# Attention's prelude in a transformer block on one core: one value product and early queries in the output product's bank, and the last chunk's row statistics in later slots

## The chip, the cores and the metric

One Trainium2 chip, one of its cores. The metric is the device time of one launch in microseconds (us), the median of several runs.

## The reference

```python
x = x + 0.5 * ffn(layernorm(x))          # x: 8 x 512 rows of 128
x = x + attn(layernorm(x))
x = x + 0.5 * ffn(layernorm(x))

def attn(x):                              # 16 heads of 64, causal; adds its own input
    q, k, v = x @ Wq, x @ Wk, x @ Wv
    s = q @ k^T / 8, masked above the diagonal
    return x + (softmax(s) @ v) @ Wo
```

`ffn` is a mixture of 32 experts (6 chosen for a row) with 16 anchors and one shared expert. The same FFN weights serve both FFN layers.

## The kernel before

The 4096 rows are worked as 8 chunks (`NC`) of 512 rows, and a chunk of 512 is one sequence of the attention. The whole is in float32 accuracy: a product is three matmuls, high part times high part, high times low and low times high (`mm3`, lines 197 to 199). A product's result in PSUM is therefore split: ScalarE writes the high part (`part_hi`, line 781, tiles `q_hi` and `k_hi`), then VectorE the low part (`part_lo`, line 1205 for `k_lo`, line 1201 for `q_lo`). Each engine has its program written out by hand, and semaphores join them.

The program is `ffn(0)`, `attention()`, `ffn(NC)`. Attention is a prelude and then 64 slots, one for each pair of heads (8 pairs in each of 8 chunks). Slot (b, p) works on several pairs at once. TensorE (PE) does, in this order:

- transposes of pair p-1's probabilities, group 1 (`probT`, line 505);
- scores of pair p+1, parts 0 and 1 (`scores`, lines 484 and 494); in their last part, behind `third_ready`, PE waits for copies of group 1;
- transposes of pair p-1, group 2;
- the keys' product of pair p+2 (K, into bank `psA`), the value product p+3 (V, into a bank of `psT`), pair p-2's output product (`project_out`, line 532, into bank `psO`), the queries' product of pair p+2 (Q, into `psA`);
- scores of pair p+1, part 2, and transposes of pair p, group 0;
- `attend` for pair p-1 (line 519, into `psA`).

The order in which the others serve this is fixed too. ScalarE (ACT) copies `psA` and half of the transposes (lines 825 and 814), makes `k_hi`, the exponentials of part 0 (`exp`, line 803), the value copy (`value_copy`, line 789), `q_hi`, and the exponentials of parts 1 and 2. VectorE (DVE) copies transposes (`pT_copy`, line 1227), takes the reciprocal of the row sums (line 1220; GpSimd then normalises, line 1358, and PE transposes), the row maxima of parts 0 and 1 (`row_max`, line 1212), `k_lo`, `q_lo`, the row maximum of part 2, and the copy of group 0.

`scores` of part u can be written when the exponentials of the part that used its banks last are done: parts share two bank pairs, so pair 1's part 1 waits for pair 0's part 2.

The prelude on PE makes the value product 0 (`psA`), K of pair 1 (bank 0 of `psT`), scores part 2 of pair 0, Q of pair 1 (bank 1 of `psT`), and then value products 1 and 2, both into `psA`, each behind the copy of the one before:

```python
                for k in (1, 2):
                    pe.wait_ge(s["v_sb"], k)
                    project_values(0, k, psA)
```

`psO` is the last bank. The FFN's last transposes lie in it until VectorE has added them (`add_y`, line 1111, semaphore `x_added`); then nothing uses it until the first output product in slot 2.

The rows' layernorm needs 1/sqrt(var + eps). In attention, the statistics of the last chunk can only be made after `add_y`: VectorE makes them in slot 0 (lines 946 to 960), ScalarE takes a square root in slot 1 (`row_std(4)`, line 690), and VectorE refines in slot 2 (`finish_std`, lines 905 to 916). A square root and an exponential need different tables on ScalarE, and the program loads a table (ACT_TABLE_LOAD) before each change. Late in attention, in chunk 5, VectorE makes such a root alone for other rows, with a seed and Newton steps (`rsqrt_seed` and `rsqrt_newton`, lines 923 to 937).

Of the kernel before, what the change touches and what calls it, by code (L numbers as in the profile page):

```python
# [32 lines left out]
TB = 4  # L33
# [12 lines left out]
RSQRT_SEED = 0x5f3759df  # L46
HP = H // 2
# [22 lines left out]
def build(nc, x_in, wg_in, wu_in, wd_in, gate_in, bias_in, wq_in, wk_in, wv_in, wo_in,  # L70
# [6 lines left out]
    with ctx:  # L77
# [171 lines left out]

        def ahead(b, p, d):  # L250

            return b + (p + d) // HP, (p + d) % HP

# [4 lines left out]
        def transposed(p, g, h=slice(0, 2)):  # L258
# [6 lines left out]
        STD = [(0, 1, 1), (1, 2, 2), (2, NC, NC), (0, NC - 1, 2 * NC - 1), (NC - 1, NC, 2 * NC),  # L265
               (2, NC, 3 * NC)]
# [82 lines left out]
        def _(pe):  # L349
# [189 lines left out]
            def attn_slot(b, p, parity, first, last):  # L539
# [29 lines left out]

                second_ready()  # L570
                if not (first and p == 0):
                    probT(*ahead(b, p, -1), 1)
                if have_s:
                    scores(*ahead(b, p, 1), 0, False)
                    scores(*ahead(b, p, 1), 1, False, third_ready)
                else:
                    third_ready()
# [66 lines left out]
            def attention():  # L644
# [40 lines left out]
        def _(act):  # L685
# [69 lines left out]
            def ffn(g0):  # L755
                ffn_chunk(g0, True, False, 2 if g0 == 0 else 5)
# [18 lines left out]
            def part_hi(b, p, which, early, special=False):  # L775
# [5 lines left out]
                nc.scalar.activation(qk[which][0][:, p % 2, :], psT[:, 1 - which, :] if early else psT[:, 1, :] if special else psA,  # L781
                                     ACT.Copy, scale=(float(DK) ** -0.5, 1.0)[which]) \
                    .then_inc(s[("q_hi", "k_hi")[which]], 1)
# [43 lines left out]
            def attn_slot(b, p, first, last):  # L827
# [22 lines left out]
                if have_q and special:  # L850
                    part_hi(*ahead(b, p, 2), 1, False, True)
# [7 lines left out]
                if p == 1 and first:  # L859
                    row_std(4)  # L860

            def attention():
# [36 lines left out]
        def _(dve):  # L899
# [20 lines left out]
            def rsqrt_seed(c):  # L920
# [3 lines left out]
                dve.wait_ge(s["rsqrt"], 1)  # L924
# [3 lines left out]
            def rsqrt_newton(c, i, last):  # L928
# [3 lines left out]
                dve.wait_ge(s["rsqrt"], 2 + 3 * i)  # L932
                tt(t, y, y, ALU.mult).then_inc(s["rsqrt"], 1)
                dve.wait_ge(s["rsqrt"], 3 + 3 * i)
                stt(out=t, in0=t, scalar=-0.5, in1=v, op0=ALU.mult, op1=ALU.mult).then_inc(s["rsqrt"], 1)
                dve.wait_ge(s["rsqrt"], 4 + 3 * i)
# [177 lines left out]
            def ffn_chunk(g, g0, first, last):  # L1114
# [50 lines left out]
                if first:  # L1165
                    finish_std(2 if g0 == 0 else 5)
# [10 lines left out]
            def a_rows(b, first, ts):  # L1177

                if not first and ts[0] == 0:
                    dve.wait_ge(s["a_xT_ps"], b)  # L1180
                normalise(b, "a_xn", ts)
# [12 lines left out]
            def part_lo(b, p, which, early, special=False):  # L1194
# [4 lines left out]
                ps = psT[:, 1 - which, :] if early else psT[:, 1, :] if special else psA  # L1199
# [36 lines left out]
            def attn_slot(b, p, first, last):  # L1236
# [15 lines left out]
                if have_q:  # L1252
                    part_lo(*ahead(b, p, 2), 1, False, special_slot(b, p))
# [17 lines left out]
                if p == 0 and first:  # L1271
                    dve.wait_ge(s["x_added"], NC)
                    chunk_stats(NC - 1, 2 * NC - 1)
                if p == 2 and first:
                    finish_std(4)
                if b == NC - 3 and p == 5:
                    rsqrt_seed(slice(0, 2 * TB))
                if b == NC - 3 and p >= 5:
                    rsqrt_newton(slice(0, 2 * TB), p - 5, p == HP - 1)
                if b == NC - 2 and p == 5:  # L1280
                    dve.wait_ge(s["rsqrt"], 11)
# [135 lines left out]
```

## Time and profile before

| | |
|---|---|
| median of 3 runs | 1490.11 us (1487.82 to 1490.38) |
| the profiled execution's own time | 1488.8 us |
| its span, first to last instruction | 1487.0 us |
| the span's parts: FFN, attention, FFN | to about 437 us, about 437 to 1083 us, from there |
| prelude, slots 0 and 1 of attention | about 437 to 465 us |

Times of rows are in us from the span's start. The times of the runs lie 1 to 3 us around the profiled one, so a difference in span is set beside the profiled execution's own time first.

### The profile page before, as it was taken

The page shows a single profiled execution, that of the slowest core. Times are in us where ns is not written, and L with a number is a line of the kernel's source. Part 1 is how long each engine was busy: PE and PEld are TensorE (multiplying, and loading weights), DVE is VectorE, ACT ScalarE, POOL GpSimd, SP SyncE. Part 2 cuts the span into 40 slices and gives each one's busy share as a digit, 9 for nine tenths or more (in the row PEclk, how much of TensorE's full clock was granted, in tenths as well). Part 3 has the DMA queues.
Part 4 walks back from the last instruction along what each step waited for, and adds up shares of the span by engine and source line. Part 5 has one row for each costly group of instructions (what it writes and reads, how often), then busy time and mean ns, then how long its engine had stood idle before and what let it go on. Part 6 is the DMA issues. An engine that isn't in the chain of part 4 may idle for free.

```text
span 1487.0 us, 28766 instructions
## 1 busy us (share of the span) xinstructions
PE 1436.2 (97%) x9664; PEld 959.0 (64%) x9664; DVE 1082.8 (73%) x2421; ACT 806.6 (54%) x1907; POOL 294.5 (20%) x589
## 2 busy tenths in 40 slices
PE   2999999999988999999999999999899999999998
PEld 1666666666655666666666666666566666666665
DVE  6977877787676666676767677767767877687775
ACT  2443334333356777777777777787644334433422
POOL 2100000000013444434443444344400000000000
PEclk9999999999999999999999999999999999999999
DMA  5343333333310000000000000000033333333332
GB/s 185 128 166 110 104 116 102 111 101 112 114 44 1 2 2 2 2 2 1 2 2 2 2 2 2 1 2 2 2 108 103 117 119 113 104 116 119 111 113 85
DMA packets 58854, 97.80 MB, mean 66 GB/s; under 512 B 6144, under 2 KB 15360, under 8 KB 58752
## 3 DMA queue, kind: packets, MB, share of 16 engines
q1 hardware_dynamic: 58752, 96.44, 20.4%
q8 instruction: 63, 1.03, 0.3%
q14 instruction: 39, 0.32, 0.1%
HBM read 92.75 MB, written 3.67 MB: 65 GB/s over the span
## 4 chain that ended last, share of the span: by engine, by line
PE 90%; DVE 5%; ACT 3%; issue 1%; DMA 1%; POOL 0%; SPq 0%; POOLq 0%; ACTq 0%; DVEq 0%
PE banks L391 19%; PE banks L197 14%; PE banks L199 13%; PE banks L198 13%; PE banks L519 9%; PE banks L484 9%; PE banks L505 5%; PE banks L532 3%; PE banks L494 2%; PE banks L353 2%; ACT work L803 1%; PE banks L363 1%; DVE work L1156 1%; DVE work L1124 1%; DVE q_lo L1201 1%
## 5 line engine op out<-in xcount | busy, mean ns | idle before, releaser
L748 ACT ACTIVATE work<-banks 128x512 f32<-128x512 f32 x336 | 200.6, 598 | 459.1 <-PE banks L199 439.4
L391 PE MATMUL banks<-work,wd 128*128 128x512 f32 x672 | 343.0, 593 | 0.3 <-DVE work L1156 0.3
L1124 DVE TENSOR_TENSOR work<-banks,work 128x512 f32<-128x512 f32 x336 | 231.9, 690 | 150.9 <-ACT work L748 146.0
L803 ACT ACTIVATE work<-banks,nmax 128x512 f32<-128x512 f32 (+3 forms) x512 | 264.0, 527 | 39.0 <-DVE nmax L1212 39.0
L1358 POOL TENSOR_SCALAR work<-work,rrec 128x512 f32<-128x512 f32 (+3 forms) x512 | 262.9, 536 | 0.0
L197 PE MATMUL banks<-xT_hi,wg_hi 128*128 (+1 forms) x336 | 248.3, 739 | 0.1
L1156 DVE TENSOR_TENSOR work<-work 128x512 f32<-128x512 f32 x320 | 226.0, 706 | 15.1 <-DVE work L1124 9.5
L1212 DVE TENSOR_REDUCE nmax<-banks 128x2 f32<-128x1024 f32 (+3 forms) x256 | 198.9, 819 | 10.8 <-PE banks L494 6.6
L1227 DVE COPY stage<-banks 128x1024 f32<-128x1024 f32 (+1 forms) x128 | 122.1, 954 | 59.0 <-PE banks L505 58.9
L391 PEld LDWEIGHTS banks<-work,wd 128*128 128x128 f32 x672 | 126.1, 189 | 34.1 <-DVE work L1156 2.7
L198 PE MATMUL banks<-xT_lo,wg_hi 128*128 (+1 forms) x336 | 133.0, 396 | 0.0
L197 PE MATMUL banks<-xT_hi,wu_hi 128*128 (+1 forms) x336 | 133.0, 396 | 0.0
L199 PE MATMUL banks<-xT_hi,wu_lo 128*128 (+1 forms) x336 | 133.0, 396 | 0.0
L198 PE MATMUL banks<-xT_lo,wu_hi 128*128 (+1 forms) x336 | 132.9, 396 | 0.0
L199 PE MATMUL banks<-xT_hi,wg_lo 128*128 (+1 forms) x336 | 132.9, 396 | 0.0
L814 ACT ACTIVATE stage<-banks 128x512 f32<-128x512 f32 x128 | 76.6, 598 | 86.7 <-PE banks L505 84.6
L505 PE MATMUL banks<-small,work 64*128 64x64 f32 x2560 | 114.7, 225 | 4.3 <-DVE stage L1227 2.7
L505 PEld LDWEIGHTS banks<-small,work 64*128 64x128 f32 x2560 | 98.3, 138 | 17.5 <-issue 16.0
L197 PEld LDWEIGHTS banks<-xT_hi,wg_hi 128*128 128x128 f32 x336 | 64.0, 191 | 67.5 <-issue 64.2
L1201 DVE SCALAR_TENSOR_TENSOR q_lo<-banks,q_hi 128x512 fp32r<-128x512 f32 x64 | 44.3, 693 | 86.8 <-ACT q_hi L781 86.8
L198 PEld LDWEIGHTS banks<-xT_lo,wg_hi 128*128 128x128 f32 x336 | 64.2, 191 | 65.3 <-issue 65.0
L803 ACT ACTIVATION_READ_ACCUMULATOR work<-banks,nmax 128x1 f32 x512 | 105.3, 206 | 0.0
(130 smaller groups left out, 2186.3 us busy)
## 6 DMA issues: line engine op xcount, KB each, us to landing
work<-cw_rows SPq DMA_DIRECT2D x320, 256.0 KB, 3.1
x<-in_x SPq DMA_DIRECT2D x8, 256.0 KB, 6.7
out_rows<-x SPq DMA_DIRECT2D x8, 256.0 KB, 2.2
cw_rows<-cwT SPq DMA_DIRECT2D x16, 96.0 KB, 1.9
stage<-in_w_gate SPq DMA_DIRECT2D x3, 448.0 KB, 5.5
stage<-in_w_up SPq DMA_DIRECT2D x3, 448.0 KB, 6.1
wd<-in_w_down SPq DMA_DIRECT2D x3, 448.0 KB, 6.8
stage<-in_wq SPq DMA_DIRECT2D x1, 512.0 KB, 4.0
```

The source lines that it names most:

```text
L197: pe.matmul(o, w[0], m[0], start=start, stop=False, skip_group_check=True)
L198: pe.matmul(o, w[0], m[1], start=False, stop=False, skip_group_check=True)
L199: return pe.matmul(o, w[1], m[0], start=False, stop=stop, skip_group_check=True)
L391: pe.matmul(psY, wd[:, j * P:(j + 1) * P], z[part_slot(j)], start=j == 0, stop=j == HT - 1, skip_group_check=True).then_inc(s["down_ps"], 1)
L484: pe.matmul(ps[:, i, o:o + w], qk[0][a][r, p % 2, qb * P:(qb + 1) * P], qk[1][c][r, p % 2, 0:w], start=qb != 0 and k == 0, stop=False, ski ...
L505: m = pe.transpose(psT[:, h, k * DK:(k + 1) * DK], prob[r, p % 2, i, o:o + P], ident[r, h * DK:(h + 1) * DK])
L748: nc.scalar.activation(silu[j % 2], psG[j % 3], ACT.Silu) \
L803: m = nc.scalar.activation(prob[:, p % 2, i, o:o + w], ps[:, i, so:so + w], ACT.Exp, bias=nmax[:, p % 2, i, qb:qb + 1], accum_out=rsum[:, ...
L1124: tt(gated[j % 3], psU[j % 3], silu[j % 2], ALU.mult) \
L1156: tt(z[part_slot(j)], gated[j % 3], spread[:, j % NSPREAD, :], ALU.mult) \
L1212: m = nc.vector.tensor_reduce(nmax[:, p % 2, :, qb], ps[:, :, o:o + (qb + 1) * P], AX.X, ALU.max, negate=True)
L1358: nc.gpsimd.tensor_scalar(t, t, rrec[:, par, i, qb:qb + 1], 1.0, ALU.mult, ALU.mult) \
```

## The change

1. `psO`, idle in the prelude, takes value product 1, which PE now makes before scores part 2; value product 2 follows Q of pair 1 directly. ScalarE makes the copy of value product 1 and `q_hi` of pair 1 before the exponentials of part 2, where they stood after.
2. Q of pairs 2 and 3 (slots 0 and 1) goes into `psO` instead of `psA`, so it doesn't wait for the low part of K. In slot 1, K waits for `k_lo` of pair 2 and no longer for `q_lo`.
3. In slot 1, PE makes scores part 0 of pair 2 before the transposes of group 1.
4. The last chunk's statistics move from slot 0 to slots 3 and 4 of chunk 0. Its root is made by VectorE alone, with seed and Newton steps in slots 5 to 7 of chunk 1; `row_std(4)`, `finish_std(4)` and their two table loads go. The counts of the semaphore `rsqrt` are adapted.

```diff
+        def part_source(n, which, early):
+            if early:
+                return psT[:, 1 - which, :]
+            if which == 1:
+                return psT[:, 1, :] if special_slot((n - 2) // HP, (n - 2) % HP) else psA
+            return psO if n < 4 else psA
...
                 # PE, attn_slot
+                if first and p == 1:
+                    scores(b, p + 1, 0, False)
                 second_ready()
                 if not (first and p == 0):
                     probT(*ahead(b, p, -1), 1)
                 if have_s:
-                    scores(*ahead(b, p, 1), 0, False)
+                    if not (first and p == 1):
+                        scores(*ahead(b, p, 1), 0, False)
                     scores(*ahead(b, p, 1), 1, False, third_ready)
...
                 elif first and p == 1:
-                    pe.wait_ge(s["q_lo"], 3)
+                    pe.wait_ge(s["k_lo"], 3)
...
-                elif have_q:
+                elif first and p == 1:
+                    pe.wait_ge(s["q_lo"], 3)
+                elif have_q and not (first and p == 0):
                     pe.wait_ge(s["k_lo"], n + 3)
                 if have_q:
-                    project(b2, p2, 0, psA)
+                    project(b2, p2, 0, part_source(n + 2, 0, False))
...
                 # PE, attention
                 project(0, 1, 1, psT[:, 0, :])
+                pe.wait_ge(s["x_added"], NC)
+                project_values(0, 1, psO)
                 scores(0, 0, 2, True)
                 pe.wait_ge(s["q_lo"], 1)
                 project(0, 1, 0, psT[:, 1, :])
-                for k in (1, 2):
-                    pe.wait_ge(s["v_sb"], k)
-                    project_values(0, k, psA)
+                pe.wait_ge(s["v_sb"], 1)
+                project_values(0, 2, psA)
...
                 # ScalarE, attn_slot and attention
-                if p == 1 and first:
-                    row_std(4)
...
                 part_hi(0, 1, 1, True)
+                value_copy(0, 1, True, psO)
+                part_hi(0, 1, 0, True)
                 exp(0, 0, 2, True)
-                part_hi(0, 1, 0, True)
-                value_copy(0, 1, True, psA)
                 value_copy(0, 2, True, psA)
...
                 # VectorE, attn_slot
-                if p == 0 and first:
+                if p == 3 and first:
                     dve.wait_ge(s["x_added"], NC)
-                    chunk_stats(NC - 1, 2 * NC - 1)
-                if p == 2 and first:
-                    finish_std(4)
+                    rows_stats(NC - 1)
+                if p == 4 and first:
+                    rows_mean(NC - 1, 2 * NC - 1)
+                if b == 1 and p == 5:
+                    rsqrt_seed(slice((NC - 1) * TB, NC * TB), 0)
+                if b == 1 and p >= 5:
+                    rsqrt_newton(slice((NC - 1) * TB, NC * TB), p - 5, p == HP - 1, 0)
```

On PE, in the prelude, the rows behind K of pair 1 were these: scores part 2 of pair 0 (banks0), Q of pair 1 (banks2), and the start of value product 1 (banks3, `aw` by `xT`).

```order
L484 MATMUL banks0<-k_hi,q_hi 128x256 x2
L484 MATMUL banks0<-k_lo,q_hi 128x256 x2
L484 MATMUL banks0<-k_hi,q_lo 128x256 x2
L484 MATMUL banks0<-k_hi,q_hi 128x256 x2
L484 MATMUL banks0<-k_lo,q_hi 128x256 x2
L484 MATMUL banks0<-k_hi,q_lo 128x256 x2
L494 MATMUL banks0<-half 128x256 x4
L197 MATMUL banks2<-xT_hi,aw_hi 128x512
L198 MATMUL banks2<-xT_lo,aw_hi 128x512
L199 MATMUL banks2<-xT_hi,aw_lo 128x512
L197 MATMUL banks3<-aw_hi,xT_hi 128x512
L198 MATMUL banks3<-aw_lo,xT_hi 128x512
```

At the same place of the changed kernel (its lines stand 1 to 14 later):

```order
L198 MATMUL banks3<-aw_hi,xT_hi 128x512
L199 MATMUL banks3<-aw_lo,xT_hi 128x512
L200 MATMUL banks3<-aw_hi,xT_lo 128x512
L492 MATMUL banks0<-k_hi,q_hi 128x256 x2
L492 MATMUL banks0<-k_lo,q_hi 128x256 x2
L492 MATMUL banks0<-k_hi,q_lo 128x256 x2
L492 MATMUL banks0<-k_hi,q_hi 128x256 x2
L492 MATMUL banks0<-k_lo,q_hi 128x256 x2
L492 MATMUL banks0<-k_hi,q_lo 128x256 x2
L502 MATMUL banks0<-half 128x256 x4
L198 MATMUL banks2<-xT_hi,aw_hi 128x512
L199 MATMUL banks2<-xT_lo,aw_hi 128x512
```

Value product 1 has moved ahead of the scores, so that only one value product is left behind Q.

On PE, from the end of slot 0 into slot 1, 32 transposes stood together (16 of pair 0's group 0, then 16 of its group 1), and all scores of pair 2 behind them:

```order
L494 MATMUL banks1<-half 128x256 x4
L505 MATMUL banks2<-small,work 128x64 x32
L484 MATMUL banks0<-k_hi,q_hi 128x512 x2
L484 MATMUL banks0<-k_lo,q_hi 128x512 x2
L484 MATMUL banks0<-k_hi,q_lo 128x512 x2
L494 MATMUL banks0<-half 128x128 x4
L484 MATMUL banks1<-k_hi,q_hi 128x384 x2
L484 MATMUL banks1<-k_lo,q_hi 128x384 x2
L484 MATMUL banks1<-k_hi,q_lo 128x384 x2
L494 MATMUL banks1<-half 128x128 x4
L505 MATMUL banks2<-small,work 128x64 x8
```

In the changed kernel:

```order
L502 MATMUL banks1<-half 128x256 x4
L513 MATMUL banks2<-small,work 128x64 x16
L492 MATMUL banks0<-k_hi,q_hi 128x512 x2
L492 MATMUL banks0<-k_lo,q_hi 128x512 x2
L492 MATMUL banks0<-k_hi,q_lo 128x512 x2
L502 MATMUL banks0<-half 128x128 x4
L513 MATMUL banks2<-small,work 128x64 x16
L492 MATMUL banks1<-k_hi,q_hi 128x384 x2
L492 MATMUL banks1<-k_lo,q_hi 128x384 x2
L492 MATMUL banks1<-k_hi,q_lo 128x384 x2
L502 MATMUL banks1<-half 128x128 x4
L513 MATMUL banks2<-small,work 128x64 x8
```

Scores part 0 of pair 2 now stands between the two groups of transposes.

On ScalarE, from the end of slot 1 into slot 2, before:

```order
L803 ACTIVATE work,rsum<-banks,nmax 128x128
L690 ACT_TABLE_LOAD
L690 ACTIVATE std<-var_eps 128x4
L825 ACTIVATE ctx_sum<-banks 128x512
L814 ACTIVATE stage<-banks 128x8x64
L814 ACTIVATE stage<-banks 128x512
L781 ACTIVATE k_hi<-banks 128x512
L803 ACT_TABLE_LOAD
L803 ACTIVATE work,rsum<-banks,nmax 128x512 x2
```

And in the changed kernel:

```order
L817 ACTIVATE work,rsum<-banks,nmax 128x128
L839 ACTIVATE ctx_sum<-banks 128x512
L828 ACTIVATE stage<-banks 128x8x64
L828 ACTIVATE stage<-banks 128x512
L795 ACTIVATE k_hi<-banks 128x512
L817 ACTIVATE work,rsum<-banks,nmax 128x512 x2
```

Both table loads and the square root are gone, and nothing stands in their place on this engine.

## Rows read from the trace of the kernel before

**Rows 1.** The page: the chain that ended last, shares of the span by engine.
```profile
PE 90%; DVE 5%; ACT 3%; issue 1%; DMA 1%; POOL 0%; SPq 0%; POOLq 0%; ACTq 0%; DVEq 0%
```

**Rows 2.** A stretch: busy PE, PEld, DVE, ACT, POOL, granted clock, DMA share, GB/s.
```profile
446.20:449.20 3.00, 3.00 (x20) 1.92 (x20) 1.18 (x1) 0.60 (x1) 3.00 (x7) 0.50 0.00 0
```

**Rows 3.** Timeline of PE, prelude into slot 0: start, us, work [idle before <-releaser].
```profile
440.68 0.39 PE L197 MATMUL banks<-aw_hi,xT_hi 128*128 128x512 f32 x1
...
445.22 0.50 PE L197 MATMUL banks<-aw_hi,xT_hi 128*128 128x512 f32 x1 [3.69 <-ACT work L789]
...
446.11 0.79 PE L484 MATMUL banks<-k_hi,q_hi 64*128 64x512 f32 x2
...
449.22 0.65 PE L197 MATMUL banks<-xT_hi,aw_hi 128*128 128x512 f32 x1
```

**Rows 4.** Timelines of DVE and ACT, prelude: add_y, row maxima, q_lo, last exponential.
```profile
437.98 0.68 DVE L1111 TENSOR_TENSOR x<-x,banks 128x512 f32<-128x512 f32 x1
...
441.42 1.01 DVE L1212 TENSOR_REDUCE nmax<-banks 128x2 f32<-128x512 f32 x2
...
444.71 0.69 DVE L1201 SCALAR_TENSOR_TENSOR q_lo<-banks,q_hi 128x512 fp32r<-128x512 f32 x1 [2.28 <-ACT q_hi L781]
...
443.98 0.21 ACT L803 ACTIVATION_READ_ACCUMULATOR work<-banks,nmax 128x1 f32 x1
```

**Rows 5.** Timeline of ACT, slot 0: k_hi.
```profile
450.37 0.60 ACT L781 ACTIVATE k_hi<-banks 128x512 fp32r<-128x512 f32 x1 [3.56 <-PE banks L199]
```

**Rows 6.** Timeline of PE: slot 1's transposes, K, attend; slot 2's scores, attend.
```profile
456.28 1.06 PE L505 MATMUL banks<-small,work 64*128 64x64 f32 x16 [1.93 <-DVE stage L1227]
...
460.30 0.50 PE L197 MATMUL banks<-xT_hi,aw_hi 128*128 128x512 f32 x1
...
465.21 2.37 PE L519 MATMUL banks<-stage,work 128*64 128x512 f32 x16
...
475.17 0.39 PE L484 MATMUL banks<-k_hi,q_hi 64*128 64x256 f32 x2 [1.08 <-ACT work L803]
...
476.87 2.37 PE L519 MATMUL banks<-stage,work 128*64 128x512 f32 x16
```

**Rows 7.** Timeline of ACT, slot 2: the load of the exponentials' table.
```profile
472.37 1.28 ACT L803 ACT_TABLE_LOAD   x1
```

**Rows 8.** Timeline of PE in one steady slot, attend to attend.
```profile
506.59 2.38 PE L519 MATMUL banks<-stage,values 128*64 128x512 f32 x16
...
508.90 0.71 PE L505 MATMUL banks<-small,work 64*128 64x64 f32 x16
...
509.42 0.48 PE L484 MATMUL banks<-k_hi,q_hi 64*128 64x512 f32 x2
...
510.30 0.43 PE L484 MATMUL banks<-k_hi,q_hi 64*128 64x384 f32 x2
...
511.03 0.42 PE L505 MATMUL banks<-small,work 64*128 64x64 f32 x8
...
511.38 0.50 PE L197 MATMUL banks<-xT_hi,aw_hi 128*128 128x512 f32 x1
...
516.30 2.37 PE L519 MATMUL banks<-stage,values 128*64 128x512 f32 x16
```

**Rows 9.** Timelines: ACT k_hi behind that K; DVE copy of group 1; slot 3's.
```profile
512.39 0.60 ACT L781 ACTIVATE k_hi<-banks 128x512 fp32r<-128x512 f32 x1 [0.30 <-PE banks L199]
...
509.65 0.69 DVE L1227 COPY stage<-banks 128x512 f32<-128x512 f32 x1 [1.20 <-PE banks L505]
...
489.61 0.69 DVE L1227 COPY stage<-banks 128x512 f32<-128x512 f32 x1 [0.61 <-PE banks L505]
```

**Rows 10.** Timeline of DVE: statistics in slot 0; seed and first Newton step in chunk 5.
```profile
456.11 0.86 DVE L948 BATCH_NORM_STATS2 bn<-x 128x6 f32<-128x128 f32 x4
...
903.76 0.16 DVE L923 TENSOR_SCALAR newton<-var_eps 128x8 uint32<-128x8 uint32 x1
...
904.57 0.17 DVE L937 SCALAR_TENSOR_TENSOR rstd<-newton,rstd 128x8 f32<-128x8 f32 x1
```

More of the change, by code:

```diff
@@ L46 @@
 RSQRT_SEED = 0x5f3759df
+RSQRT_STEPS = 11
 HP = H // 2
@@ L263, in transposed @@
             return dst[:, :, h, :], src
-        STD = [(0, 1, 1), (1, 2, 2), (2, NC, NC), (0, NC - 1, 2 * NC - 1), (NC - 1, NC, 2 * NC),
-               (2, NC, 3 * NC)]
+        STD = [(0, 1, 1), (1, 2, 2), (2, NC, NC), (0, NC - 1, 2 * NC - 1), (2, NC, 3 * NC)]
         XT, LOGITS, YT, CWT = 2, 5, 8, 18
@@ L755, in ffn @@
             def ffn(g0):
-                ffn_chunk(g0, True, False, 2 if g0 == 0 else 5)
+                ffn_chunk(g0, True, False, 2 if g0 == 0 else 4)
                 with act.Fori(g0 + 1, g0 + NC - 1) as g:
@@ L773, in a_xT_high, with part_hi @@
                     .then_inc(s["a_xT_hi"], 1)
-            def part_hi(b, p, which, early, special=False):
+            def part_hi(b, p, which, early):
                 n = pair(b, p)
@@ L780, in part_hi @@
                     act.wait_ge(s["s_ps"], 3 * n - 3)
-                nc.scalar.activation(qk[which][0][:, p % 2, :], psT[:, 1 - which, :] if early else psT[:, 1, :] if special else psA,
+                nc.scalar.activation(qk[which][0][:, p % 2, :], part_source(n, which, early),
                                      ACT.Copy, scale=(float(DK) ** -0.5, 1.0)[which]) \
@@ L850, in attn_slot @@
                 if have_q and special:
-                    part_hi(*ahead(b, p, 2), 1, False, True)
+                    part_hi(*ahead(b, p, 2), 1, False)
                 if p == 1 and not first:
@@ L918, in finish_std, with rsqrt_seed, rsqrt_newton @@
                 dve.wait_ge(s["stat_dve"], k + 5)
-            def rsqrt_seed(c):
+            def rsqrt_seed(c, done):
                 v, y, t = [a[:, c].bitcast(U32) for a in (var_eps, rstd0, newton)]
                 nc.vector.tensor_scalar(t, v, 1, None, ALU.logical_shift_right).then_inc(s["rsqrt"], 1)
-                dve.wait_ge(s["rsqrt"], 1)
+                dve.wait_ge(s["rsqrt"], done + 1)
                 nc.vector.tensor_scalar(y, t, -1.0, float(RSQRT_SEED), ALU.mult, ALU.add) \
                     .then_inc(s["rsqrt"], 1)
-            def rsqrt_newton(c, i, last):
+            def rsqrt_newton(c, i, last, done):
                 v, y, t = [a[:, c] for a in (var_eps, rstd0, newton)]
                 stt = nc.vector.scalar_tensor_tensor
-                dve.wait_ge(s["rsqrt"], 2 + 3 * i)
+                dve.wait_ge(s["rsqrt"], done + 2 + 3 * i)
                 tt(t, y, y, ALU.mult).then_inc(s["rsqrt"], 1)
-                dve.wait_ge(s["rsqrt"], 3 + 3 * i)
+                dve.wait_ge(s["rsqrt"], done + 3 + 3 * i)
                 stt(out=t, in0=t, scalar=-0.5, in1=v, op0=ALU.mult, op1=ALU.mult).then_inc(s["rsqrt"], 1)
-                dve.wait_ge(s["rsqrt"], 4 + 3 * i)
+                dve.wait_ge(s["rsqrt"], done + 4 + 3 * i)
                 stt(out=rstd[:, c] if last else y, in0=t, scalar=1.5, in1=y, op0=ALU.add, op1=ALU.mult) \
@@ L1165, in ffn_chunk @@
                 if first:
-                    finish_std(2 if g0 == 0 else 5)
+                    finish_std(2 if g0 == 0 else 4)
             def ffn(g0):
@@ L1180, in a_rows @@
                     dve.wait_ge(s["a_xT_ps"], b)
+                    if b == NC - 1:
+                        dve.wait_ge(s["rsqrt"], RSQRT_STEPS)
                 normalise(b, "a_xn", ts)
@@ L1192, in a_xT_low, with part_lo @@
                     .then_inc(s["a_xT_lo"], 1)
-            def part_lo(b, p, which, early, special=False):
+            def part_lo(b, p, which, early):
                 n = pair(b, p)
@@ L1198, in part_lo @@
                 hi, lo = [t[:, p % 2, :] for t in qk[which]]
-                ps = psT[:, 1 - which, :] if early else psT[:, 1, :] if special else psA
+                ps = part_source(n, which, early)
                 if which == 0:
@@ L1252, in attn_slot @@
                 if have_q:
-                    part_lo(*ahead(b, p, 2), 1, False, special_slot(b, p))
+                    part_lo(*ahead(b, p, 2), 1, False)
                 if p == 2 and not first:
@@ L1270, in attn_slot @@
                     a_residual(b + 1)
-                if p == 0 and first:
+                if p == 3 and first:
                     dve.wait_ge(s["x_added"], NC)
-                    chunk_stats(NC - 1, 2 * NC - 1)
-                if p == 2 and first:
-                    finish_std(4)
+                    rows_stats(NC - 1)
[5 more added lines that the diff above has]
+                    rsqrt_newton(slice((NC - 1) * TB, NC * TB), p - 5, p == HP - 1, 0)
                 if b == NC - 3 and p == 5:
-                    rsqrt_seed(slice(0, 2 * TB))
+                    rsqrt_seed(slice(0, 2 * TB), RSQRT_STEPS)
                 if b == NC - 3 and p >= 5:
-                    rsqrt_newton(slice(0, 2 * TB), p - 5, p == HP - 1)
+                    rsqrt_newton(slice(0, 2 * TB), p - 5, p == HP - 1, RSQRT_STEPS)
                 if b == NC - 2 and p == 5:
-                    dve.wait_ge(s["rsqrt"], 11)
+                    dve.wait_ge(s["rsqrt"], 2 * RSQRT_STEPS)
                     dve.wait_ge(s["a_xT_ps"], NC)
```

## The prediction, written before the run

> **What bounds the kernel now.** I read the page first. The chain that ended last is 90% on TensorE (PE) [rows 1], so a stall counts where PE stands still, and PE's lost time anywhere moves all that follows. Next I read PE's timeline over one slot in the middle of attention. From one attend to the next it takes 9.71 us (506.59 to 516.30), and no idle time is marked on it [rows 8]. A slot can't be shortened by shortening another engine's work, but it shows what a slot costs when nothing is waited for. The third view is PE's timeline from the prelude into slot 2, held against that.
>
> There three places lose time. First, PE waits 3.69 us in the prelude for the copy of value product 1, before it can put value product 2 in the same bank [rows 3]. Second, after that wait the granted clock is 0.50, the lower level of 1.2 GHz, from about 446.2 to 449.2 [rows 2]. Scores parts 0 and 1 then take 3.11 us (446.11 to 449.22) [rows 3], against 1.61 us (509.42 to 511.03) at 2.4 GHz [rows 8]. A second wait of 1.93 us, for VectorE's copy of group 0, is followed by the same: 16 transposes last 1.06 us [rows 6] where they last 0.71 [rows 8]. From these transposes to slot 1's K it is 4.02 us (456.28 to 460.30) [rows 6], against 2.48 (508.90 to 511.38) [rows 8]. Third, slot 2 takes 11.66 us, attend to attend (465.21 to 476.87), and has a wait of 1.08 us for exponentials [rows 6]; they stand behind a table load of 1.28 us that starts at 472.37 [rows 7].
>
> **The change, step by step.** I follow PE, and give each step as the distance from before.
>
> Prelude. PE makes the same five products and scores up to value product 2, in another order. Value product 1 waits for add_y, which ends at 438.66 [rows 4]; PE is at that point at about 438.5 (estimated: 440.68 less the 1.95 us or so of scores part 2 and Q, less the wait), so this costs 0.2 at most. Value product 2 then starts about where value product 1's end was, 440.68 plus 0.8, at 441.5, as its bank was copied long before. It ends near 442.5. Q of pair 1 is ready before that, at about 441.7, and ScalarE, free of the exponentials of part 2 by the new order, has q_hi by 442.3 (0.61 us each). VectorE is in the row maxima until 442.43 and then needs 0.69 us for q_lo: 443.1 [rows 4]. Scores part 0 of pair 1 start there, and not at 446.11 [rows 3]: 3.0 earlier. PE's wait is now 0.6 to 0.7 us, not 3.69.
>
> Part 1 of pair 1 waits for the last exponential of pair 0. That ends at 444.19 as before (443.98 + 0.21) [rows 4], because its row maxima haven't moved. Part 1 then takes 0.73 us (510.30 to 511.03) [rows 8], and K of slot 0 starts at 444.96, not 449.22 [rows 3]: **4.26 earlier**. That includes the first stretch at the lower clock, which I expect to be gone.
>
> Slot 0. k_hi follows the start of K after 1.01 us (511.38 to 512.39) [rows 8, 9]: 445.97 instead of 450.37 [rows 5], 4.40 earlier. From there to the first transposes of slot 1 the chain is k_hi, exponentials, value copy, q_hi, q_lo, row maxima, copy of group 0. It is on ScalarE and VectorE and hasn't changed inside: 5.91 us (450.37 to 456.28) [rows 5, 6]. Q in `psO` comes earlier on PE, but the exponentials of part 0 are what scores part 2 waits for, so I give this nothing. The statistics that left slot 0 stood behind the copy of group 0; their cover was the time in which PE was transposing, so nothing again. The transposes of group 1 start at 451.9: **4.4 earlier**.
>
> Slot 1. Scores part 0 of pair 2 (0.88 us, 509.42 to 510.30 [rows 8]) now lies inside that wait. It needs exponentials that are done near 450.1, so it ends near 451.0 and is free. Behind the transposes (0.71 us [rows 8]) comes the copy of group 1 (0.69 us [rows 9]), for which the end of part 1 waits, then 0.1 to 0.2 of masks, then transposes of group 2 (0.35 us, 511.03 to 511.38 [rows 8]). K starts about 1.95 us after the transposes, against 4.02: **2.05 more**. In this the higher clock and the moved scores can't be told apart, since the copy's chain is the bound either way. From K to attend it was 4.91 us (460.30 to 465.21) [rows 6], of which PE waited for k_lo before Q. That wait goes, but the exponentials and q_lo, which follow K, set attend's start; I take **0.1**, between 0 and 0.4.
>
> Slot 2. Without the two loads (the other one, as long, with its root, stood at the end of slot 1 in front of the copy of ctx and of the transposes) the slot should be a steady one: 11.66 less 9.71, **1.95 more**. The Trainium skill ("ScalarE: Activation LUTs", What ACT_TABLE_LOAD costs) gives a switch of tables as the load of 1.28 us plus a drain of about 1.38, 2.66 in all. The trace shows the load alone: k_hi's end, the load and the exponential follow each other without a gap. By the page two switches would take 5.3 us from ScalarE, and slot 2 couldn't have lost only 1.95; the sum is unchanged by it.
>
> The moved rows. Statistics in slot 3 are 0.86 us [rows 10] and a small copy, behind the residual. VectorE has 0.61 us idle there before the copy of group 1 [rows 9]: that copy comes some 0.3 late. It was done 0.4 to 0.5 us before PE asks for it (copy from 509.65 for 0.69, masks of part 1 just before 511.03 [rows 8, 9]), so nothing, or at most 0.2. The means in slot 4 are about as much (0.8, an estimate from the 0.86) in 1.20 us of idle time [rows 9]. The seed and first step are five dependent instructions, 0.98 us from the first start to the last end (903.76 to 904.57, plus 0.17) [rows 10], in the same 1.20 us; later steps are three. If the cover were gone, they would cost 0.98 and twice about 0.6, 2.2 us in all. I take 0, with 0 to 0.5. The wait for the root, in front of the last chunk's normalisation, lies some forty slots behind it.
>
> Sum: 4.4 + 2.05 + 0.1 + 1.95 = **8.5 us**. From slot 3 on PE is bound by its own work, nothing in attention waits for a transfer, and the second FFN hangs on attention's end alone, so the whole goes through. The profiled execution took 1488.8 us with a span of 1487.0, so the same execution would read 1480.3 with a span of 1478.5. The median of the runs lies 1.3 above the profiled one: 1490.1 less 8.5 is **1481.6**.
>
> **The rivals.** *The lower clock comes in the new prelude too.* Speaking for it: the changed prelude still has three waits on PE of 0.5 to 0.9 us within 9 us, and PE is mostly doing short scores. Against: in slot 2 a wait of 1.08 us [rows 6] left the clock alone, and both drops followed waits of 1.93 and 3.69 us [rows 3, 6]. One drop costs up to 1.5 us (3.11 less 1.61, or 4.02 less 2.48), part of it inside waits: 1482.5 to 1483.1, and two make 1484.6. Chance 0.17.
>
> *The moved statistics and Newton steps are not covered.* They delay copies of group 1 and the row sums' reciprocal, which starts GpSimd's normalisation. Against it: the row 903.76 and those behind it stood in just such a slot, and the copy after them was on time. By the bounds above 0.5 to 2.2 us: 1482.1 to 1483.8. Chance 0.07.
>
> *The time is given back.* A chain that the early start doesn't move (SyncE's transfers, GpSimd, or an exponential behind a new row) takes PE over in slots 2 to 7. I see none: GpSimd is idle between slots, and the prelude's other chain, the row maxima to 442.43 and the last exponential to 444.19, is already in the sum. If only step 1 or only slot 2 remained, 2 to 4 us: 1486 to 1488. Chance 0.06.
>
> *Slower.* The order on ScalarE is the place: q_hi of pair 1 now stands before the exponentials of part 2, and every slot is in strict order. Should VectorE's added rows hold up q_lo or the copies in each of the five slots they stand in, PE would lose there. To reach 1493.1 (0.2% above) it must lose 11.5 us, 2.3 in each, where the rows added are 0.6 to 1.0 us. Chance 0.02.
>
> That the change doesn't do what it says is nearly excluded: the program's order shows both loads gone, and the rows moved.
>
> **How the numbers follow.** The forecast, the full 8.5 with 0.5 on either side for the steps' estimates, has a chance of 0.68, and the runs of the kernel before spread over 2.6 us, so its own range is 1479.3 to 1483. To the first two rivals the range goes up to 1485; below, the runs' lowest (1487.8) less 9.0 is 1478.8. About what a measurement of this kernel can tell from no change is 0.2%, 3 us. Faster by more than that is below 1487.1: the forecast, the first two rivals and half of the third, less a little for what I haven't seen: 0.93. Within it 0.05, slower 0.02.
>
> **What the profile will show.** Right: PE's longest wait between 438 and 452 is under 1 us; the granted clock is 1.00 throughout; scores part 0 of pair 1 start near 443.1, K of slot 0 near 445.0, K of slot 1 near 453.8, attend near 458.7; no table load between prelude and attention's end; slot 2 lasts 9.7; slots 3 to 7 of chunk 0, and 5 to 7 of chunk 1, last as before. Wrong: a clock of 0.50 anywhere there; a wait for the copy of group 1 in slots 3, 13, 14 or 15; attend in slot 2 reached less than 7 us earlier. The prediction falls if q_lo of pair 1 isn't ready until after the exponentials, or if attention's end is reached with less lead than slot 3's start had.

## The result and the profile after

The changed kernel takes 1482.19 us (median of 5 runs, 1480.2 to 1483.36), beside 1489.93 us for the kernel before (5 runs). The ratio is 0.995, with a 95% interval of 0.9938 to 0.9962: 5.7 to 9.2 us less. The profiled execution took 1482.46 us, with a span of 1480.7 us. Its granted clock was 1.00 in every microsecond from 20 us on.

The span is 6.3 us shorter, where 8.5 were forecast, so the first question is where 2.2 us are. VectorE's first instruction waits for the first loads. Its row before, and then the one after (start, us, work, idle time before and what ended it):

```profile
7.08 0.15 DVE L946 COPY pace<-small 128x1 f32<-128x1 f32 x1 [7.08 <-DMA bias<-in_gate_bias]
```

```profile
9.29 0.15 DVE L958 COPY pace<-small 128x1 f32<-128x1 f32 x1 [9.29 <-DMA bias<-in_gate_bias]
```

A load that the change doesn't touch landed 2.2 us later in this execution, and all the rest of the first FFN is moved by it: attention's first scores stand at 437.04 and not at 434.83. In all twelve profiles of this document 427.6 to 427.8 us lie between that row and the first scores, so it is the landing alone that moves them. From here on I count every time from those scores, and write it with a plus sign: +8.3 is 8.3 us after them. Then PE's timeline after answers [rows 3, 6]:

```profile
437.04 0.50 PE L492 MATMUL banks<-k_hi,q_hi 64*128 64x512 f32 x2 [0.55 <-DVE q_lo L1215]
...
445.33 0.50 PE L492 MATMUL banks<-k_hi,q_hi 64*128 64x512 f32 x2 [0.71 <-DVE q_lo L1215]
...
447.29 0.50 PE L198 MATMUL banks<-xT_hi,aw_hi 128*128 128x512 f32 x1
...
450.28 0.39 PE L492 MATMUL banks<-k_hi,q_hi 64*128 64x256 f32 x2 [0.64 <-ACT work L817]
...
452.47 0.50 PE L492 MATMUL banks<-k_hi,q_hi 64*128 64x512 f32 x2 [0.49 <-ACT work L817]
...
454.14 0.71 PE L513 MATMUL banks<-small,work 64*128 64x64 f32 x16 [0.57 <-DVE stage L1241]
...
456.04 0.50 PE L198 MATMUL banks<-xT_hi,aw_hi 128*128 128x512 f32 x1
...
459.03 0.39 PE L492 MATMUL banks<-k_hi,q_hi 64*128 64x256 f32 x2 [0.56 <-ACT work L817]
...
460.73 2.38 PE L527 MATMUL banks<-stage,work 128*64 128x512 f32 x16
...
470.44 2.37 PE L527 MATMUL banks<-stage,work 128*64 128x512 f32 x16
```

In the prelude, VectorE and ScalarE show what PE waits for there (answers [rows 4]): row maxima, q_lo behind them without a gap, and the last exponential of part 2.

```profile
443.62 1.02 DVE L1226 TENSOR_REDUCE nmax<-banks 128x2 f32<-128x512 f32 x2
444.58 0.69 DVE L1215 SCALAR_TENSOR_TENSOR q_lo<-banks,q_hi 128x512 fp32r<-128x512 f32 x1
...
446.18 0.21 ACT L817 ACTIVATION_READ_ACCUMULATOR work<-banks,nmax 128x1 f32 x1
```

The waits of 3.69 and 1.93 us are gone, and what is left are five of 0.49 to 0.71 us, for q_lo, for exponentials and for VectorE's copy. Scores part 0 of pair 1 stand at +8.3 (+11.3 before), attend of slot 1 at +23.7 (+30.4), attend of slot 2 at +33.4 (+42.0), and the span ends at +1043.7 (+1052.2): 8.5 us less from there. In stretches of 10 us the clock reads 1.00 (busy time of PE, weight loads, VectorE, ScalarE, GpSimd; then clock, DMA share and GB/s):

```profile
436.00:446.00 10.00, 8.63 (x63) 5.50 (x61) 5.93 (x9) 8.10 (x22) 0.00 (x0) 1.00 0.01 2
446.00:456.00 10.00, 8.17 (x103) 5.98 (x99) 6.72 (x11) 7.22 (x24) 4.49 (x11) 1.00 0.00 0
```

The moved rows on VectorE, in slot 3 of chunk 0 and in slot 5 of chunk 1, each with the copy of group 1 behind them (which answers [rows 9]):

```profile
482.58 0.86 DVE L960 BATCH_NORM_STATS2 bn<-x 128x6 f32<-128x128 f32 x4
483.36 0.67 DVE L1241 COPY stage<-banks 128x512 f32<-128x512 f32 x1
...
581.82 0.16 DVE L949 SCALAR_TENSOR_TENSOR rstd<-newton,rstd 128x4 f32<-128x4 f32 x1
582.31 0.69 DVE L1241 COPY stage<-banks 128x512 f32<-128x512 f32 x1 [0.32 <-PE banks L513]
```

In slot 3 the copy has no idle time before it: it starts 0.2 us after the transposes' end (482.44 plus 0.71), and PE doesn't wait for it. In slot 5, 0.32 us of idle time are left. From attend to attend PE takes 9.70 us in slot 3 (9.68 before), and 9.69 to 9.71 in slots 13 to 16 (9.68 to 9.71 before). PE's idle time in none of these slots is for VectorE's copy.

### The profile page after: what moved, and what is told of

Read it like the earlier page. It is cut to its first block, busy times and chain, and to the rows that moved or that the text cites. A ratio compares the mean times of both kernels' runs of the same rounds, so it can differ in the third digit from the quotient of the medians.

```text
span 1480.7 us, 28770 instructions
## 1 busy us (share of the span) xinstructions
PE 1432.6 (97%) x9664; PEld 956.6 (65%) x9664; DVE 1082.4 (73%) x2427; ACT 803.3 (54%) x1904; POOL 294.2 (20%) x589
## 4 chain that ended last, share of the span: by engine, by line
PE 90%; DVE 5%; ACT 2%; issue 1%; DMA 1%; POOL 0%; SPq 0%; POOLq 0%; ACTq 0%; DVEq 0%
PE banks L399 19%; PE banks L198 14%; PE banks L200 13%; PE banks L199 13%; PE banks L527 10%; PE banks L492 9%; PE banks L513 6%; PE banks L540 3%; PE banks L502 2%; PE banks L361 2%; ACT work L817 1%; PE banks L371 1%; DVE work L1136 1%; DVE work L1168 1%; DVE q_lo L1215 1%
## 5 line engine op out<-in xcount | busy, mean ns | idle before, releaser
L817 ACT ACTIVATE work<-banks,nmax 128x512 f32<-128x512 f32 (+3 forms) x512 | 263.7, 527 | 37.6 <-DVE nmax L1226 37.5
```

The source lines that it names most:

```text
L817: m = nc.scalar.activation(prob[:, p % 2, i, o:o + w], ps[:, i, so:so + w], ACT.Exp, bias=nmax[:, p % 2, i, qb:qb + 1], accum_out=rsum[:, ...
```

## The experiments

Nine kernels ran, the kernel before three times and the changed one twice, which makes twelve profiles. In this table all distances are from the same scores, in each run's profile. The lower clock is where the granted clock reads 0.50, up to the last matmul; the last column is the median time in us, with the number of runs.

| kernel | first scores | attend slot 1 | attend slot 2 | span's end | lower clock, us from the span's start | median time |
|---|---|---|---|---|---|---|
| before | 434.83 | +30.4 | +42.0 | +1052.2 | 446.2 to 449.6, 456.4 to 459.8 | 1489.93 (5) |
| before_again | 435.69 | +31.4 | +43.0 | +1053.2 | 445.0 to 451.8, 458.7 to 462.1 | 1490.82 (1) |
| before_third | 434.83 | +31.4 | +43.0 | +1053.2 | 444.1 to 450.9, 457.7 to 461.2 | 1489.82 (1) |
| changed | 437.04 | +23.7 | +33.4 | +1043.7 | none | 1482.19 (5) |
| after_again | 435.87 | +23.7 | +33.4 | +1045.1 | 1069.1 to 1072.5 | 1482.79 (1) |
| a_prelude_only | 435.29 | +24.6 | +36.2 | +1046.4 | none | 1484.56 (5) |
| b_stats_only | 436.68 | +28.8 | +38.5 | +1048.7 | 447.5 to 451.0 | 1488.43 (10) |
| c_no_early_scores | 436.45 | +24.2 | +34.0 | +1045.8 | 1070.0 to 1073.5 | 1482.71 (4) |
| d_q_in_psA | 436.13 | +24.0 | +33.7 | +1046.9 | 1068.9 to 1075.8 | 1484.84 (1) |
| e_old_act_order | 436.82 | +27.9 | +37.6 | +1047.8 | 446.5 to 453.3 | 1484.64 (4) |
| g_all_but_stats | 435.64 | +24.3 | +36.1 | +1046.4 | none | 1483.11 (4) |
| h_exp_before_k | 435.55 | +22.9 | +32.6 | +1044.4 | 1067.7 to 1071.2 | 1481.68 (5) |

**a_prelude_only**: of the diff, only the prelude's lines.

```diff
                 project(0, 1, 1, psT[:, 0, :])
+                pe.wait_ge(s["x_added"], NC)
+                project_values(0, 1, psO)
                 scores(0, 0, 2, True)
...
+                value_copy(0, 1, True, psO)
+                part_hi(0, 1, 0, True)
                 exp(0, 0, 2, True)
...
```

> Only the prelude's part of the change (value product 1 in the idle bank, ScalarE's order there); queries in psA, scores and statistics as before. Distances are counted from attention's first scores (434.83 in the trace before, 437.04 in the changed kernel), since the two executions reached them 2.2 us apart. My theory: the wait of 3.69 us goes, and with it the stretch at the lower clock behind it; scores part 0 of pair 1 stand at +8.3 and not +11.3, K of slot 0 at +10.2 and not +14.4, attend of slot 1 at about +26.0 and not +30.4 (4.2 to 4.6 gained), and this is kept to the end. The second wait of some 2 us before slot 1's transposes stays, and the lower clock behind it. Rival (the clock is not set by that wait): the stretch at 0.50 stays or moves, and 3.0 are gained. Rival (only the changed steps together gain): under 1.5.

PE's timeline of it:

```profile
435.29 0.50 PE L493 MATMUL banks<-k_hi,q_hi 64*128 64x512 f32 x2 [0.55 <-DVE q_lo L1211]
...
443.58 0.49 PE L493 MATMUL banks<-k_hi,q_hi 64*128 64x512 f32 x2 [0.72 <-DVE q_lo L1211]
...
452.44 0.71 PE L514 MATMUL banks<-small,work 64*128 64x64 f32 x16 [1.92 <-DVE stage L1237]
...
454.94 0.50 PE L198 MATMUL banks<-xT_hi,aw_hi 128*128 128x512 f32 x1
...
459.85 2.38 PE L528 MATMUL banks<-stage,work 128*64 128x512 f32 x16
```

The scores came at +8.3 as expected, but 5.8 us were gained at attend of slot 1 and not 4.4. The row of 452.44 says why. The wait of 1.92 us is there as before, and yet the 16 transposes behind it last 0.71 us, where before they lasted 1.06 [rows 6]: the clock stayed up. So this wait doesn't bring the lower clock by itself, and my forecast had taken it that it does. The time was 1484.56 us (1483.07 to 1487.11), ratio 0.9966 (0.9951 to 0.998). In its five runs the time follows the mean granted clock of the whole execution: 1483.07 and 1483.46 us at 1.000, 1484.56 at 0.999, 1485.81 at 0.998, 1487.11 at 0.996.

**b_stats_only**: of the diff, only the statistics, the root and what belongs to them.

```diff
-                if p == 1 and first:
-                    row_std(4)
...
+                if p == 3 and first:
+                    rows_stats(NC - 1)
+                if b == 1 and p == 5:
+                    rsqrt_seed(slice((NC - 1) * TB, NC * TB), 0)
...
```

> Only the last chunk's statistics and root moved; prelude, queries and scores as before. My theory: attend of slot 1 stays at +30.4, slot 2 falls from 11.66 to 9.7, so 1.95 gained at the end, and nothing more. Rival (a switch of tables costs more than the load's row): 3 to 5 gained. Rival (the loads are hidden, or the moved rows on VectorE cost as much): 0 to 0.5 gained.

```profile
458.12 0.71 PE L513 MATMUL banks<-small,work 64*128 64x64 f32 x16 [1.93 <-DVE stage L1235]
...
465.51 2.37 PE L527 MATMUL banks<-stage,work 128*64 128x512 f32 x16
...
475.21 2.37 PE L527 MATMUL banks<-stage,work 128*64 128x512 f32 x16
```

Slot 2 takes 9.70 us (465.51 to 475.21), 1.96 less than before, as expected: two loads and a root are worth that on PE's path, and not the 3 to 5 of the rival. But attend of slot 1 stands at +28.8 and not at +30.4 as expected. The span's end comes 3.45 us earlier, counted from the first scores (+1048.7 for +1052.2), and the other 1.5 of these are the clock again. The same wait of 1.93 us has full-speed transposes behind it; from them to attend it is 7.39 us, against 8.93 (456.28 to 465.21) [rows 6]. The time was 1488.43 us (10 runs, 1485.52 to 1491.8), ratio 0.9993 (0.9982 to 1.0004). So the times don't show the 1.96 us: the interval holds no change too, and these ten runs had a mean clock of 0.9970, lower than the 0.9977 of the kernel before. The gain of this step is read from the trace alone.

**before_again** and **before_third**: no edit.

> The kernel before once more, unchanged. If the stretches at the lower clock are the program's (the same waits bring them each time), its profile shows two, at +11.3 and +21.5, and attend of slot 1 at +30.4. If they differ from one execution to the next, as the changed kernels' profiles suggest (a wait of 1.92 us without one, one of 1.60 us with one), attend of slot 1 lies anywhere from +27.3 (none) to +30.4 (two), in steps of about 1.5, and the mean clock between 1.000 and 0.998 with it.

> The kernel before a third time. If the wait of 3.7 us brings the lower clock in every execution and the wait of 1.9 us in some: one stretch at 0.50 starting between +9.8 and +12, a second one or none, attend of slot 1 at +28.8 to +31.4. If the first is chance as well: +27.3 is possible.

Before_again's attend of slot 1 stands at +31.4, outside what either case had allowed (+27.3 to +30.4), because a stretch can be twice as long as the one I had seen. Before_third's lies in the range given for it. The row behind the long wait in before_again, and windows with columns as above:

```profile
446.06 0.80 PE L197 MATMUL banks<-aw_hi,xT_hi 128*128 128x512 f32 x1 [3.67 <-ACT work L789]
```

```profile
446.00:451.00 5.00, 4.94 (x24) 3.06 (x25) 1.70 (x4) 0.61 (x2) 4.24 (x9) 0.50 0.00 0
459.00:462.00 3.00, 3.00 (x28) 2.21 (x26) 2.59 (x11) 0.56 (x1) 1.62 (x4) 0.50 0.03 5
```

The first matmul behind the wait takes 0.80 us here and 0.50 in the first profile [rows 3]: the clock was already down. The first stretch lasted 3.4 us in one execution and 6.8 in the two others, and attend of slot 1 moved with it, from +30.4 to +31.4. Without both stretches it would be 3.11 less 1.61, and 8.93 less 7.39, earlier than +30.4: about +27.4, an estimate, as no profile of this kernel ran without them. Beside that figure the step of the prelude alone (+24.6) is worth 2.8 us, and the clock in the profile before 3.0.

**e_old_act_order**: the changed kernel with ScalarE's old order in the prelude.

```diff
-                value_copy(0, 1, True, psO)
-                part_hi(0, 1, 0, True)
                 exp(0, 0, 2, True)
+                part_hi(0, 1, 0, True)
+                value_copy(0, 1, True, psO)
```

> The changed kernel, but ScalarE in the prelude as before: exponentials of part 2, then q_hi of pair 1 and the copy of value product 1. PE has its value products early and then waits for q_lo. If the bank alone were the gain: nothing lost. My theory: scores part 0 of pair 1 stand at about +10.6 (q_lo's old place, 445.40 less 434.83) against +8.3, so 2.3 lost there, less the 0.15 of the wait for the exponentials; the wait is 2.8 us in one piece, and if it brings the lower clock, another 1.5 lost: attend of slot 1 at +25.8 without and +27.3 with it.

```profile
447.44 0.80 PE L492 MATMUL banks<-k_hi,q_hi 64*128 64x512 f32 x2 [3.06 <-DVE q_lo L1215]
...
464.67 2.37 PE L527 MATMUL banks<-stage,work 128*64 128x512 f32 x16
```

```profile
446.50:453.50 7.00, 6.07 (x27) 4.36 (x28) 3.61 (x5) 2.39 (x7) 4.26 (x9) 0.51 0.00 0
```

The idle bank by itself moves PE's wait and hardly shortens it: 3.69 us for the copy become 3.06 for q_lo. The scores start at +10.6, 2.3 later, and the lower clock comes, here for 6.8 us; together 4.2 us lost at attend of slot 1 (+27.85, where I had expected +27.3 with the lower clock). With the bank alone the scores come 0.7 us earlier than before (+10.6 for +11.3), and with the order on ScalarE too 3.0. The order without the bank wasn't run. The time was 1484.64 us (4 runs, 1482.09 to 1486.37).

**c_no_early_scores**: scores part 0 of pair 2 behind the transposes again.

```diff
-                if first and p == 1:
-                    scores(b, p + 1, 0, False)
                 second_ready()
...
-                    if not (first and p == 1):
-                        scores(*ahead(b, p, 1), 0, False)
+                    scores(*ahead(b, p, 1), 0, False)
...
```

> The changed kernel, but scores part 0 of pair 2 behind slot 1's transposes, as before. PE then waits some 2.1 us in one piece for the copy of group 0. If the clock holds: 0.5 us lost (the steady slot's 2.48 from transposes to K against 1.90 measured), attend of slot 1 at +24.2. If a wait of that length brings the lower clock, as the 1.93 us did before: 2.0 lost, attend at +25.7. The rival that early scores are worth nothing: +23.7.

```profile
453.54 0.68 PE L513 MATMUL banks<-small,work 64*128 64x64 f32 x15 [2.15 <-DVE stage L1238]
...
456.01 0.50 PE L198 MATMUL banks<-xT_hi,aw_hi 128*128 128x512 f32 x1
...
460.70 2.37 PE L527 MATMUL banks<-stage,work 128*64 128x512 f32 x16
...
1070.04 1.12 PE L513 MATMUL banks<-small,work 64*128 64x64 f32 x16 [1.60 <-POOL work L1373]
```

0.56 us lost at attend of slot 1 (+24.25 against +23.69), with the clock up behind a wait of 2.15 us. It is lost between the transposes and K: 2.47 us here (453.54 to 456.01), 1.90 in the changed kernel. At attention's end, behind a wait of only 1.60 us that every one of these programs has, 16 transposes took 1.12 us: there the clock was down, in a place that the edit doesn't touch. That is the other 1.5 us in this row of the table, which ends 2.1 us later than the changed kernel's. The time was 1482.71 us (4 runs, 1482.38 to 1483.98).

**d_q_in_psA**: Q of pairs 2 and 3 in `psA` behind k_lo again.

```diff
-            return psO if n < 4 else psA
+            return psA
...
-                elif first and p == 1:
-                    pe.wait_ge(s["q_lo"], 3)
-                elif have_q and not (first and p == 0):
+                elif have_q:
                     pe.wait_ge(s["k_lo"], n + 3)
...
```

> The changed kernel with Q of pairs 2 and 3 in psA again, behind k_lo. The waits for k_lo (0.7 us each before) come back in front of Q, but scores part 2 behind Q then wait less for exponentials. My theory: 0.25 lost in each of slots 0 and 1, attend of slot 1 at +24.2. Rival (it is worth what the waits were): 1.3 lost, +25.0. Rival (nothing): +23.7.

0.28 us lost at attend of slot 1 (460.10 less 436.13 is +23.97): half of what I expected, and far from what the waits for k_lo last, 0.72 and 0.64 us in this profile. They stand in place of the waits of 0.64 and 0.56 us for exponentials that the changed kernel has behind Q. The one run took 1484.84 us, with the lower clock for 6.8 us at attention's end.

**g_all_but_stats**: statistics, root and table loads as before.

```diff
+                if p == 0 and first:
+                    chunk_stats(NC - 1, 2 * NC - 1)
...
+                if p == 1 and first:
+                    row_std(4)
...
```

> The changed kernel with the last chunk's statistics, square root and table loads as before. Distances from attention's first scores. If each step stands by itself: scores part 0 of pair 1 at +8.3, attend of slot 1 at +23.7 as in the changed kernel, slot 2 11.6 instead of 9.7, 1.95 lost to the end. If the statistics behind the copy of group 0 in slot 0 now matter (VectorE is nearer to the path than before): up to 0.5 more lost, in slot 1. Granted clock: with few long waits a mean of 0.999 to 1.000, if the stretches at 0.50 belong to the long waits that the other steps remove.

```profile
454.10 0.68 DVE L1242 COPY stage<-banks 128x512 f32<-128x512 f32 x1
...
454.84 0.23 PE L503 MATMUL banks<-half 64*128 64x128 bf16 x2 [0.70 <-DVE stage L1242]
...
459.94 2.37 PE L528 MATMUL banks<-stage,work 128*64 128x512 f32 x16
...
471.74 2.38 PE L528 MATMUL banks<-stage,work 128*64 128x512 f32 x16
```

2.7 us lost: 0.6 in slot 1 (+24.3) and 2.1 in slot 2 (11.80 us against 9.71), where I had expected up to 0.5 and 1.95. The 0.6 are the statistics behind the copy of group 0. They now hold up the copy of group 1, which starts at +18.5 where it was +17.8 in the changed kernel (454.88 less 437.04), and PE's last masks of part 1 wait 0.70 us for it. All four of its runs had a mean clock of 1.000, and took 1482.57 to 1483.75 us. Their median, 1483.11, is 0.9 us above the changed kernel's: the times of four or five runs don't show a step of 2.7 us in its size.

**h_exp_before_k**: a step further. In slots 0 and 1 ScalarE makes the exponentials of part 0 before k_hi.

```diff
-                if have_q and not special:
+                if have_q and not special and not (first and p < 2):
                     part_hi(*ahead(b, p, 2), 1, False)
                 if have_s:
                     exp(*ahead(b, p, 1), 0, first and p == 0)
+                if first and p < 2:
+                    part_hi(*ahead(b, p, 2), 1, False)
```

> The changed kernel, and in slots 0 and 1 ScalarE makes the exponentials of part 0 before k_hi (it waits for K's product while row maxima are already there). My theory: the chain on ScalarE in slot 0 starts 0.5 us earlier, in slot 1 0.2 more: attend of slot 1 at +23.0, 0.7 less to the end. Rival (k_lo and q_lo come later and give it back): +23.7 or more. The times of runs spread over 2 to 3 us, so the distances in the trace decide.

```profile
458.46 2.37 PE L527 MATMUL banks<-stage,work 128*64 128x512 f32 x16 [0.38 <-DVE q_lo L1217]
```

Attend of slot 1 stands at +22.9 and of slot 2 at +32.6, 0.8 us earlier than in the changed kernel, where 0.7 was expected. Attend now waits 0.38 us for q_lo, which the exponentials were moved ahead of. The time was 1481.68 us (5 runs, 1479.43 to 1482.14), ratio 0.9943 (0.9929 to 0.9957). It is the fastest by the trace; the times alone don't separate it from the changed kernel.

**after_again**: the changed kernel, no edit.

> The changed kernel once more, unchanged, for what belongs to an execution and not to the program. If attention's first scores come 2.2 us later because of the program, they stand at 437.0 again; if that is the first load's landing, anywhere from 434.8 to 437. From there, attend of slots 1 and 2 at +23.7 and +33.4 again in either case, if the steps of the change are the program's; a stretch at the lower clock may fall on the waits of 0.8 and 1.6 us at attention's end, where other profiles have shown it, and none on the prelude.

```profile
8.20 0.15 DVE L958 COPY pace<-small 128x1 f32<-128x1 f32 x1 [8.20 <-DMA bias<-in_gate_bias]
...
459.57 2.37 PE L527 MATMUL banks<-stage,work 128*64 128x512 f32 x16
```

Attention began at 435.87, and attend of slots 1 and 2 stood at +23.7 and +33.4, to 0.02 us as in the first profile. The steps are the program's; the 2.2 us at the start (here 1.0 of them) and the stretch of lower clock at 1069 to 1072.5 are the execution's.

## Why the prediction was right, and where it wasn't

The time lies in the range (1478.8 to 1485.0) and 0.6 us above the forecast of 1481.6. The medians lie 7.7 us apart, and the two profiled executions 6.3, since the load landed later in the second. From attention's first scores on, the forecast of each step can be laid beside the trace by taking 434.83 from it.

- Prelude: scores part 0 of pair 1 forecast at +8.3, measured +8.3; K of slot 0 at +10.1, measured +10.25 (447.29 less 437.04), as part 1 took 0.85 us (446.44 to 447.29) and not 0.73. (By its own terms the forecast's 444.96 should have been 444.92.) The chain was the named one: row maxima, then q_lo.
- Slot 0: transposes at +17.1, measured +17.1. Slot 1: K at +19.0, measured +19.0; attend at +23.9, measured +23.7: from K to attend it was 4.69 us for 4.91, 0.2 gained where 0.1 was said. Slot 2: 9.7, measured 9.71.
- Sum: 8.5, measured 8.6 at attend of slot 2 and 8.5 at the span's end. The moved rows cost nothing that the slots' lengths show, as forecast, with the copy of slot 3 0.2 us late where 0.3 was said. The 0.1 between goes in small steps over the whole of attention, and before_again set beside before shifts by up to 0.1 there too.

Three things in it were not right, though none moved the result out of the range.

- *What the clock is.* The forecast counted about 3 us of the two stretches at 0.50 as the program's, and expected them gone because the waits go. For the long wait that held: it, or one of 3.06 us, came with the lower clock in 5 profiles of 5 (before three times, b, e). For the wait of 1.9 to 2.2 us it was 3 of 6: before three times, but not a, b and c. So 3.0 of the 8.5 us between the two profiles hang on the clock in the one profile of before, and beside before_again or before_third they would have been 4.0. That the sum came out to the tenth is in this part luck: both stretches happened to be there, at their shorter length. The runs agree with it on average only. In 23 runs of the kernel before, the mean clock was 0.9977, with an average time of 1489.7 us, and in the changed kernel's five it was 0.9996. Times 1487, that difference is 2.8 us, if each percent of clock is a percent of time; the rest of the gain is what the program's order gives. Three of the 23 runs read 0.999 (1487.43, 1487.62 and 1488.01 us), which is the mean that b's profile has with one stretch of 3.4 us, where the first profile of before, with two, has 0.998. So not every execution of the kernel before has two.
- *"So nothing again"* for the statistics leaving slot 0. From slot 1's transposes to K it is 2.50 us in a, which keeps them, and 2.47 in c, which doesn't, so where the scores stand behind the transposes they do cost nothing. But the forecast didn't look for what they would cost beside early scores: 0.6 us in slot 1 (g). In the sum it made no difference, as the sum was for the statistics gone.
- *"Can't be told apart"* for early scores and clock in slot 1, "since the copy's chain is the bound either way". It isn't: from transposes to K it was 4.02 us before, 2.47 to 2.50 in a, b and c, at the higher clock with all scores behind the transposes, and 1.90 in the changed kernel. Of the 2.1 us gained there 1.5 are the clock and 0.6 the early scores.

Single steps don't add up here: undone one at a time, early scores, Q in `psO` and statistics in slot 0 cost 0.56, 0.28 and 0.61 at attend of slot 1, 1.45 together, but all three undone (a) cost 0.87. They shorten the same chain. Q in `psO`, which the forecast put at nothing in slot 0, is a term of 0.28 us over both slots.

The rival of the lower clock in the new prelude (0.17) didn't come in any profile that had all the prelude's steps (changed twice, a, c, d, g, h); where in the two slowest runs of a, at 0.998 and 0.996, the clock fell isn't known. That of uncovered rows and that of time given back are refuted by the slots' lengths.

Around the two table loads before, ScalarE's rows were these, with the second load, from 472.37 to 473.65 [rows 7], between the last two:

```profile
467.71 1.28 ACT L690 ACT_TABLE_LOAD   x1
469.01 0.21 ACT L690 ACTIVATE std<-var_eps 128x4 f32<-128x4 f32 x1
...
471.75 0.60 ACT L781 ACTIVATE k_hi<-banks 128x512 fp32r<-128x512 f32 x1 [0.30 <-PE banks L199]
...
473.66 0.69 ACT L803 ACTIVATE work<-banks,nmax 128x512 f32<-128x512 f32 x1
```

Each load starts and ends within 0.02 us of its neighbours. The Trainium skill ("ScalarE: Activation LUTs", What ACT_TABLE_LOAD costs) gives a drain of about 1.38 us with each switch of tables. These rows have no room for it, and here they decide.

What stays open: whether the second stretch before comes only where the first did. In three profiles of before both came, and in b the first alone; that is too few. And why the same wait comes with the lower clock in one execution and not in the next, no run here shows.

## What to carry to other kernels

A bank freed for a product only moves the wait, if the engine that must read the results still takes them in the old order: follow the chain to the next consumer and reorder that too. Compare profiles from a common event, not from the span's start, and look at the clock of each microsecond before counting a slow stretch as the program's. Where work is removed beside a chain that other steps shorten, cost it against the new chain, not the old.

## What the runs showed of the hardware

The wait of 1.60 us at attention's end stood in all twelve profiles with the same surroundings, and came with the lower clock in four (c, d, h, after_again), for 3.4 us in three and 6.8 in one. The same program can have it or not, and it costs 1.5 to 3 us each time.

The twelve stretches in the table have one of two lengths, 3.4 us or 6.8. In the four long ones the clock fell while PE was still waiting, 0.6 to 1.1 us before the wait's end (before_again, before_third and e in the prelude, d at attention's end). In the eight short ones it fell when the wait ended or up to 0.9 us after it. In attention no wait of 1.1 us or less had one behind it.

The first loads' landing differed by up to 2.2 us between executions (7.08 to 9.29 us), which moved attention's first scores between 434.83 and 437.04. Between the three profiles of the kernel before, these two account for the whole difference: before_third's span is 1.0 us longer than the first's by the longer stretch alone, and before_again's 1.9, 1.0 by the stretch and 0.9 by the landing. That they also make the spread of the other runs is likely but not shown.
